# Expert adapter kernel: where W_up, ln_w and ln_b are loaded from, and where the end of the sort runs

## What is computed

```python
Wd = W_down[stream]; bd = b_down[stream]; Wu = W_up[stream]; bu = b_up[stream]
g = ln_w[stream]; b = ln_b[stream]
h = jnp.einsum('bsh,bhk->bsk', hidden_states, Wd) + bd[:, None, :]   # 512 -> 256
h = jax.nn.gelu(h, approximate=False)
h = jnp.einsum('bsk,bkh->bsh', h, Wu) + bu[:, None, :]               # 256 -> 512
h = residual + h
mean = jnp.mean(h, axis=-1, keepdims=True)
var = jnp.mean(jnp.square(h - mean), axis=-1, keepdims=True)
h = (h - mean) * jax.lax.rsqrt(var + LN_EPS)
return h * g[:, None, :] + b[:, None, :]
```

## Time and profile before

| | us |
|---|---|
| median of 3 runs | 144.26 |
| lowest and highest | 143.03 to 144.78 |
| profiled execution, its own time | 145.15 |
| span of the profiled execution | 143.4 |
| PE busy in the span | 128.3 (90%) |
| DVE, POOL, ACT busy | 114.0, 102.8, 84.2 |

### The profile page before, as it was taken

The page is one execution under the profiler, slowest core; times in us unless marked ns, Lnnn a source line. Parts: engine busy times, 40 slices in busy tenths (PEclk is TensorE's granted clock), DMA queues, the critical chain, the costliest instruction groups (busy, mean ns, idle before and its releaser), DMA issues.

```text
span 143.4 us, 4070 instructions
## 1 busy us (share of the span) xinstructions
PE 128.3 (90%) x840; PEld 113.4 (79%) x841; DVE 114.0 (80%) x278; ACT 84.2 (59%) x175; POOL 102.8 (72%) x112
## 2 busy tenths in 40 slices
PE   6899786948699999999999999999999999999830
PEld 6798655817499999999989899999989889998610
DVE  2789492497988788888897888888888888888982
ACT  1645585424576666666666666666666666666600
POOL 6021950507298988888889897988888889889870
PEclk9999999999999999999999999999999999999995
DMA  1967899993203345554543455444455633331365
GB/s 46 347 200 245 249 269 281 287 253 109 73 7 110 112 146 154 158 149 138 178 145 118 163 186 160 138 141 170 146 174 148 151 74 91 77 84 39 91 167 150
DMA packets 13200, 21.94 MB, mean 153 GB/s; under 512 B 2297, under 2 KB 3842, under 8 KB 13186
## 3 DMA queue, kind: packets, MB, share of 16 engines
q1 hardware_dynamic: 8514, 14.17, 34.6%
q10 hardware_dynamic: 4672, 7.62, 17.8%
HBM read 13.39 MB, written 8.65 MB: 154 GB/s over the span
## 4 chain that ended last, share of the span: by engine, by line
PE 65%; DMA 11%; DVE 8%; SPq 4%; issue 4%; DVEq 3%; POOL 2%; ACT 1%; POOLq 1%; ACTq 0%
PE hg_ps L811 27%; PE y_ps L844 25%; PE xT_ps L797 8%; DMA lnw_rows<-in_L_cond_ln_w_dram 6%; PE hg_ps L820 4%; DMA wu<-in_L_cond_W_up_dram 4%; SPq L240 2%; POOL res L386 2%; DMA itok_all_i<-in_itok_B_dram 2%; DVEq L608 1%; DVE hb L638 1%; DVE r_stats L650 1%; DVE slot_same L726 1%; DVEq L61 1%; DVE scaled L671 1%
## 5 line engine op out<-in xcount | busy, mean ns | idle before, releaser
L386 POOL TENSOR_TENSOR res<-normed,lnb_rows 128x512 f32<-128x512 f32 x31 | 40.0, 1289 | 19.5 <-ACT normed L464 19.3
L369 POOL TENSOR_TENSOR xb<-x_sb,bu_rows 128x512 f32<-128x512 f32 x33 | 43.6, 1324 | 4.1 <-ACT bu_rows L475 4.1
L444 ACT ACTIVATE g<-hb 128x256 f32<-128x256 f32 x33 | 13.8, 418 | 40.4 <-DVE hb L638 40.4
L650 DVE BATCH_NORM_STATS2 r_stats<-y_ps 128x6 f32<-128x512 f32 x33 | 23.0, 697 | 8.9 <-issue 8.6
L671 DVE SCALAR_TENSOR_TENSOR scaled<-y_ps,r_mv,lnw_rows 128x512 f32<-128x512 f32 x33 | 24.5, 744 | 2.1 <-DMA lnw_rows<-in_L_cond_ln_w_dram 2.0
L844 PE MATMUL y_ps<-wu_hi,gT_hi 128*128 x66 | 23.5, 436 | 2.2 <-ACT gT_hi L449 2.1
L811 PE MATMUL hg_ps<-wd_hi,xT_hi 128*128 x132 | 23.9, 303 | 0.3 <-ACT xT_hi L439 0.3
L630 DVE TENSOR_TENSOR xT_lo<-xT_ps,xT_hi 128x512 fp32r<-128x512 f32 x33 | 22.8, 690 | 0.4 <-ACT xT_hi L439 0.2
L375 POOL TENSOR_TENSOR rstd<-var_eps,half_neg 128x1 f32<-128x1 f32 x33 | 18.1, 549 | 6.5 <-DVE var_eps L659 6.5
L844 PE MATMUL y_ps<-wu_hi,gT_lo 128*128 x66 | 21.0, 399 | 1.9 <-DVE gT_lo L644 1.9
L464 ACT ACTIVATE normed<-scaled,rstd 128x512 f32<-128x512 f32 x31 | 22.4, 723 | 0.0
(11 more groups left out here) (83 smaller groups left out, 150.8 us busy)
## 6 DMA issues: line engine op xcount, KB each, us to landing
x_sb<-in_x_dram SPq DMA_DIRECT2D x64, 128.0 KB, 2.9
out_dram<-res ACTq DMA_DIRECT2D x33, 128.0 KB, 2.4
out_dram<-res SPq DMA_DIRECT2D x33, 128.0 KB, 2.5
wd<-in_L_cond_W_down_dram ACTq DMA_DIRECT2D x3, 512.0 KB, 4.8
wu<-in_L_cond_W_up_dram SPq DMA_DIRECT2D x3, 512.0 KB, 5.1
lnw_rows<-in_L_cond_ln_w_dram ACTq DMA_DIRECT2D x1, 768.0 KB, 8.7
lnb_rows<-in_L_cond_ln_b_dram ACTq DMA_DIRECT2D x1, 768.0 KB, 10.0
x_sb<-in_x_dram ACTq DMA_DIRECT2D x2, 128.0 KB, 2.6
```

Of the source, the lines that this page charges most:

```text
L369: pool.tensor_tensor(xb[:, c % DEEP, :], x_sb[:, c % FAR, :], bu_rows[:, ds(e * H, H)], ALU.add).then_inc(xb_ready, 1)
L386: pool.tensor_tensor(res[:, c % FAR, :], normed[:, c % PAR, :], lnb_rows[:, ds(e * H, H)], ALU.add).then_inc(res_ready, 1)
L650: dve.bn_stats(r_stats[:, c % DEEP, :], y_ps[c % YBANKS][:]).then_inc(stats_ready, 1)
```

## The change

`load_w_up` now loads expert e into place e, without a table: expert 0 from ACT's queue behind W_down, experts 1 and 2 from SP right behind the first rows. One semaphore, `wu_in`, counts all three. Which expert fills slot i is looked up when the halves are made: a small table `wu_from` is read into three registers on ACT and on DVE, and `wu_high` and `wu_low` read `wu` at an address from a register. ACT waits for all three loads (`wu_in` at 48) ahead of its first `wu_high`.

`ln_w` is loaded by SP behind tile 2, `ln_b` behind tile 4; ACT issues neither any more. The sort's tail stands on DVE behind x_lo(0). down_bias(0) now stands ahead of x_lo(1), gelu(0) ahead of seed(0), and on PE transpose_x(1) behind down(0). The last warm-up is one product and not two. The rows of tiles 0 and 1 are loaded by two queues, one half each, in both kernels.

```diff
-    WARM_UPS = 9, 3, 2
+    WARM_UPS = 9, 3, 1
-        wu_in = [sem(f"wu_in{e}") for e in range(E)]
+        wu_in = sem("wu_in")
+        def load_w_up(eng, e):
+            eng.dma_start(wu[:, e, :, :], w_up[e].rearrange("(c p) n -> p c n", p=P)).then_inc(wu_in, 16)
+        def w_up_part(source):
+            return wu[:].rearrange("p e c n -> p (e c n)")[:, ds(source * (KB * H), KB * H)]
+        def w_up_sources(eng, regs):
+            eng.reg_load(regs, wu_from[0:1, 0:E])
+            return [eng.snap(reg, min_val=0, max_val=E - 1 - slot) + slot for slot, reg in enumerate(regs)]
 # SP
-            sp.wait_ge(slots_ready, 2)
-            sp.reg_load(head_regs, io_table[0:1, 5:9])
-            load_w_up(sp, 0, sp.snap(head_regs[0], min_val=0, max_val=E - 1))
-            load(2, 2, [sp.snap(reg, min_val=0, max_val=B - 1) for reg in head_regs[1:3]])
...
-            load_w_up(sp, 2, third)
+            for e in range(1, E):
+                load_w_up(sp, e)
+            load(2, 2, entries(2, 0, 2))
+            sp.dma_start(lnw_rows[:], rows_of(ln_w, P)).then_inc(lnw_in, 16)
+            for t in range(3, 5):
+                load(t, t, entries(t, 0, 2))
+            sp.dma_start(lnb_rows[:], rows_of(ln_b, P)).then_inc(lnb_in, 16)
 # ACT
             for e in range(E):
                 load_w_down(act, e)
+            load_w_up(act, 0)
...
+            act.wait_ge(slots_ready, 2)
+            sources = w_up_sources(act, source_regs)
             x_hi(0, 0)
             keep_up_bias(2)
             x_hi(1, 1)
+            gelu(0, 0)
             seed(0, 0)
-            wu_high(0)
-            gelu(0, 0)
+            act.wait_ge(wu_in, 16 * E)
+            wu_high(0, sources[0])
             g_hi(0, 0)
             x_hi(2, 2)
-            wu_high(1)
-            act.dma_start(lnw_rows[:], rows_of(ln_w, P)).then_inc(lnw_in, 16)
+            wu_high(1, sources[1])
 # DVE
             x_lo(0, 0)
-            x_lo(1, 1)
+            dve.tensor_copy(key_f[:], key_filled[:])
+            link(dve.tensor_scalar(slot_batch[:], key_filled[:, 1:1 + SLOTS], B - 1, None, ALU.bitwise_and))
...
+            dve.tensor_copy(io_view[:, STORE_A_LAG:, 2], slot_store[:, 0:SLOTS:2]).then_inc(slots_ready, 1)
             dve.wait_ge(bd_ready, len(bd_banks))
             down_bias(0, 0)
+            x_lo(1, 1)
-            wu_low(0)
+            wu_low(0, sources[0])
 # PE
             transpose_x(0, 0)
-            transpose_x(1, 1)
             pe.wait_ge(wd_hi_ready, E - 1)
...
             down(0, 0, expert_of(pe, 0))
+            transpose_x(1, 1)
```

More of the change, by code:

```diff
@@ L74, in adapter_program @@
         top_row = sb("top_row", [1, E], I32)
+        wu_from = sb("wu_from", [1, E], I32)
         ones = sb("ones", [P, P])
@@ L465, in rescale, with wu_high @@
                                scale=rstd[:, c % DEEP:c % DEEP + 1]).then_inc(normed_ready, 1)
[L467 to L470, removed]
+            def wu_high(slot, source):
+                act.copy(wu_hi[:, slot * KB * H:(slot + 1) * KB * H], w_up_part(source)).then_inc(wu_hi_ready, 1)
             def keep_up_bias(e):
@@ L475, in keep_up_bias @@
                 act.copy(bu_rows[:, e * H:(e + 1) * H], y_ps[e][:]).then_inc(bu_ready, 1)
-            head_regs = [act.alloc_register(f"act_head{i}") for i in range(4)]
+            source_regs = [act.alloc_register(f"act_source{i}") for i in range(E)]
             w_down_high(act, 0).then_inc(wd_hi_ready, 1)
@@ L481, in _ @@
             act.copy(biases_hi[:], biases[:]).then_inc(biases_hi_ready, 1)
+            head_regs = [act.alloc_register(f"act_head{i}") for i in range(4)]
             act.wait_ge(slots_ready, 1)
@@ L513, in _ @@
             body(1, 1)
-            wu_high(2)
-            act.dma_start(lnb_rows[:], rows_of(ln_b, P)).then_inc(lnb_in, 16)
+            wu_high(2, sources[2])
             for t in range(2, STORE_B_LAG):
@@ L625, in _ @@
             dve.wait_ge(slots_ready, 2)
+            sources = w_up_sources(dve, near_regs[:E])
             def x_lo(t, c):
@@ L682, in shift_last, with wu_low @@
                                          op0=ALU.mult, op1=ALU.add).then_inc(last_ready, 1)
-            def wu_low(e):
-                dve.wait_ge(wu_hi_ready, e + 1)
-                w_up_low(dve, e).then_inc(wu_lo_ready, 1)
-            x_lo(0, 0)
-            x_lo(1, 1)
+            def wu_low(slot, source):
+                part = slice(slot * KB * H, (slot + 1) * KB * H)
+                dve.wait_ge(wu_hi_ready, slot + 1)
+                dve.tensor_tensor(wu_lo[:, part], w_up_part(source), wu_hi[:, part].bitcast(F32),
+                                  ALU.subtract).then_inc(wu_lo_ready, 1)
+            x_lo(0, 0)
+            dve.tensor_copy(key_f[:], key_filled[:])
+            link(dve.tensor_scalar(slot_batch[:], key_filled[:, 1:1 + SLOTS], B - 1, None, ALU.bitwise_and))
+            link(dve.tensor_copy(slot_batch_f[:], slot_batch[:]))
+            link(dve.tensor_tensor(slot_same[:], key_f[:, 1:1 + SLOTS], key_f[:, 0:SLOTS], ALU.is_equal))
+            link(dve.scalar_tensor_tensor(out=slot_store[:], in0=slot_same[:], scalar=float(B), in1=slot_batch_f[:],
+                                     op0=ALU.mult, op1=ALU.add))
+            dve.tensor_copy(io_view[:, STORE_A_LAG:, 2], slot_store[:, 0:SLOTS:2]).then_inc(slots_ready, 1)
             dve.wait_ge(bd_ready, len(bd_banks))
             down_bias(0, 0)
-            wu_low(0)
+            x_lo(1, 1)
+            wu_low(0, sources[0])
             g_lo(0, 0)
@@ L695, in _ @@
             x_lo(2, 2)
-            wu_low(1)
+            wu_low(1, sources[1])
             def body(t, c):
@@ L719, in _ @@
             body(1, 1)
-            wu_low(2)
+            wu_low(2, sources[2])
             body(2, 2)
[L723 to L729, removed]
             for t in range(3, 6):
```

16 lines of the change are left out of this document (1 added, 15 removed).

## The result

The changed kernel takes 143.48 us (median of 20 runs, 141.21 to 146.26), the kernel before 144.37 (median of 20, 142.49 to 146.05). The direction was right, though 0.9 us is small beside the spread of either kernel; 143.48 lies above the stated range of 138.6 to 142.4, and the 4.0 us of gain came out as 0.9.

A forecast was written before the change was run, and what follows sets the result against it. PE bounds tiles 4 to 30 at 3.49 us each, so only tile 4's start can move: 2.0 + 2.34 - 0.6 + 0.3 = 4.0 us off the median 144.26 gives 140.3, range 138.6 to 142.4.

The forecast's parts named there:

- Edits at nothing: Head: one warm-up product less and row halves behind W_up on ACT's queue; 0.3 gain to about 0.5 loss, taken as nothing.
- ln_w: DVE at scale(0): the early load removes the wait for ln_w and moves tile 3's turn forward; worth 2.0 us.
- Tail in the middle: DVE between scale(1) and tile 2's statistics: moving the sort's tail away gains 2.34 us, then PE bounds at 3.49 a tile.
- Tail in the head: DVE behind x_lo(0): tail stopped once by POOL, down_bias(0) two us later at 16.65, g_hi(0) 1.3 later at 19.0.
- rule of two inputs: DVE beside POOL: a DVE operation whose two inputs lie in SBUF stands still until POOL's operation is done.
- the second rival: Head: tail stopped twice, slot_same and slot_store each by a POOL add; another 1.3 us, gain 2.7, 141.6; chance 0.15.
- Collision of wu_low(2): DVE behind x_lo(3): wu_low(2) now runs into POOL's add_bias(4); cost 0.6 us, between nothing and 1.3.
- W_up: ACT from g_hi(0) to g_hi(1): no 1.6 us of waiting for W_up, g_hi(1) at 23.85, 0.3 us earlier.
- The slower one, the joint wait: ACT ahead of first wu_high: waits for all three experts, each us past 18.05 costs one; 145.6 if landing at 23.4; chance 0.06.
- late rows of tile 3: PE ahead of transpose_x(3): at 206 GB/s rows 3.3 us behind, 143.6; at 225 GB/s gain 2.0, 142.3; chance 0.12.
- The forecast's condition for W_up: Head: 2.10 MB from 8 us there by 18.05; 16.7, 15.7 or 18.2 by rate; judged met, slowest on the edge.
- the middle class: Whole kernel: a measured time within 2% (2.9 us) of the kernel before, no change told; chance 0.26.

The follow-up runs named there:

- after_again: The changed kernel once more, unaltered: 142.9 us (12 runs), beside the kernel before at 143.62.
- after_third: The changed kernel unaltered, in another series: 143.0 us (seven runs), beside the kernel before at 143.79.
- after_warm8: The changed kernel with eight products in the last warm-up: 144.0 us (6 runs).
- before_warm1: The kernel before with one warm-up product fewer (WARM_UPS 9, 3, 1), nothing else changed: 144.18 us, ratio 1.005.
- tail_back: The changed kernel with the sort's tail put back between body(2) and body(3) on DVE: 147.13 us (12 runs), before 144.15.
- sp_tail_fill: Changed kernel with expert 0 on SP, the tail behind down_bias(0) and x_lo(1), and added warm-up products keeping PE filled; read for time alone: 143.44 us (12 runs).
- sp_tail_later_b: Second series of the changed kernel with expert 0 on SP and the sort's tail behind down_bias(0) and x_lo(1) on DVE: 143.48 us (12 runs).
- after: The changed kernel itself, first measurement: 143.48 us (median of 20); its profiled execution took 141.21 us.
- after_warm2: The changed kernel with the second warm-up product put back (WARM_UPS 9, 3, 2): 142.57 us.
- wu0_on_sp: The changed kernel with expert 0 of W_up issued by SP behind its halves of tiles 0 and 1, not by ACT: 142.07 us (first series, six runs).
- after_warm16: The changed kernel with sixteen products in the last warm-up: 143.01 us (12 runs).

## Why the forecast was wrong

**The failed step.** It is the one under "Edits at nothing": that the halves of tiles 0 and 1 behind 0.52 MB of W_up cost at most 0.5 us, taken at nothing. They landed between 11.4 and 13.7 us. At 11.4, in the profiled execution, that cost nothing: tile 4's turn is at 34.15 where 34.0 was forecast. At 12.1, in after_again, it is 0.7 us later, and at 13.0 with the low clock, in after_third, 3.7 us later, nearly the whole gain. The forecast had the numbers and didn't use them: it divided 2.10 MB by the rate for W_up, and 3.41 MB for tile 3, but gave the first rows no such sum. At 8 us ACT's queue held 0.52 + 0.26 MB ahead of the last of its rows. If the two queues share the DMA engines evenly, SP's 0.26 + 1.05 MB move beside them, and the halves are there after 1.3 to 1.6 MB, which at 274 GB/s is 4.7 to 5.7 us, 13 us or so. That sum has the size and would have given the warning, but it is not how the queues shared: by 12 us ACT's queue had moved 2.35 of its 2.38 MB and SP's 0.36 to 0.40, both in the execution whose half landed at 11.41 and in after_warm8, whose half landed at 13.73. What was still missing then was a few packets, 2074 and 2079 of 2096 being done, and why they came so much later in the one than in the other stays open. The half clock on top of the lateness, worth 2.1 us, was in no rival.

**The second error: the base.** All 4.0 us were taken from the median, though they had been sized on one execution 0.9 above it. Taken off that execution's 145.15 they give 141.15, and none of the 39 executions of the changed kernel is shorter than 141.21: the 140.3 lay below all of them. So of the 3.2 us between 140.3 and 143.48 this step is 0.9, and 2.3 are the executions' distance from the shortest. With expert 0 on SP's queue the median is 142.0, which gives about 1.5 of the 2.3 to the load on ACT's queue, with eleven executions on two other chips as the evidence; the rest stays open. Even where the clock was whole, at 0.97 or more, the changed kernel was only 1.5 to 2.5 us under the median of the kernel before in its three series, not 4.0.

**What held.** *ln_w*: no wait at scale(0), as forecast; but the 2.0 us vary (1.6 in before_warm1), and no run shows the early load by itself to be worth them. *Tail in the middle*: forecast 2.34, measured 2.2 (tail_back against after_again), PE taking over as bound at 3.47 us a tile. *Tail in the head*: down_bias(0) forecast at 16.65, measured 16.56; g_hi(0) 19.0 and 19.25; g_hi(1) 23.85 and 24.00. The way there was another than assumed: slot_same slipped in ahead of POOL's add, slot_store was stopped (1.24 us), and the copy behind it too (1.16; 0.18 in the earlier trace rows), which has one input and so lies outside the forecast's rule of two inputs. So the tail was stopped twice, as in the second rival, and not once. That down_bias(0) came out right to 0.1 us is luck: the 1.16 us that the forecast had put behind the copy for the register load did not come on top of the second stop. *Collision of wu_low(2)*: forecast 0.6, measured 1.81 - 1.21 = 0.6. The Trainium skill's page SBUF — State Buffer, section Who interferes with whom, has the rule that POOL's reads of SBUF stop DVE's operations with two SBUF inputs; the 1.24 agrees. *W_up*: ACT did not wait for it in the profiled execution.

**The rivals.** The slower one, the joint wait, was real but waited behind another bound: it decided only once the rows and the tail were out of its way. PE waited for late rows of tile 3 in sp_tail_fill alone, 0.47 us; those of tile 2, which no rival named, came late there (2.11 us) and in sp_tail_later_b (1.31). The forecast's condition for W_up was also read too kindly: at 206 GB/s it gives 18.2 against the 18.05 that were needed. The low chance for the middle class (0.26 within 2%) came from the missing case of late first rows.

The best of the kernels tried is the changed one with expert 0 of W_up on SP: 142.0 us at the median of eleven, against 143.8 and 144.15 for the kernel before in the two series, a ratio of 0.99.

## What to carry to other kernels

When a load is put ahead of others in a queue, make the sum of bytes for everything behind it, first of all for what the first product waits for, and take the worst sharing of the queues as the bound. A load in the head that lands late costs its lateness and, where PE idles meanwhile, the clock: hold PE busy to the latest landing or move the load. Size a gain on the median by at least two profiles, or take it off the execution that it was read from and say how far that stands from the median.

## What the hardware showed

A DMA of 128 KB, issued at the same time (7.86 to 7.99 us) behind the same transfers, took 3.42, 4.17, 5.00 and 5.87 us to land in four executions (after, after_again, after_third, after_warm8) of kernels whose transfers are alike up to there; in the kernel before the halves on that queue took 2.6 at the median. The same idle time of PE did not always bring the low clock: 1.73 us of it did not in after_warm2, 1.34 did in the changed kernel's profiled execution. It came without late rows too, as from 9 to 11 us in wu0_on_sp. At the low clock the four transposes of the first tile took 1.09 us (after_third) and at the full one 0.60 (after_warm16). DVE's copy and cast of 33 and 66 elements on one partition took 1.16 and 1.19 us beside a POOL add, 0.18 without.
